# Softmax attentions of a decoder on one core: the order of steps picked by a running estimate of engines, banks and operands

## The reference

```
# layer 0, "mixed": 16 heads of 16; own keys (causal) and the context's keys, both added
y  = softmax(causal(q k^T * scale)) v
y += softmax(qc kc^T * scale) vc            # kc, vc of the 1601 context rows
x  = LN(x + y Wp + bp)
# layer 1: _mha twice, 16 heads of 32, each followed by an MLP
a = softmax(q k^T / sqrt(32));  if causal: a = a * (t > s)   # mask after the softmax
x_out = x + (a v) li1_w + li1_b
```

## Time and profile before

| what | value |
|---|---|
| median of 3 runs | 3924.6 us (3923.4 to 3930.83) |
| the profiled execution | 3913.16 us, its span 3911.8 us |
| linear attention, up to about | 205 us |
| mixed attention | 205 to 1250 us |
| experts and state space | 1250 to 1511 us |
| a1 | 1511 to 2036 us |
| its MLP | 2036 to 2184 us |
| a2 | 2184 to 3203 us |
| its MLP, feed-forward | 3203 to 3912 us |
| PE busy | 3400.6 us, 87% of the span |

### The profile page before, as it was taken

How to read it: one execution, slowest core, us unless ns; L and a number is a source line. 1 busy time by engine, 2 the same in 40 slices (tenths; PEclk the granted TensorE clock), 3 DMA queues, 4 the chain that set the end, 5 groups by cost and what they waited for, 6 DMA issues and landing times. The chain is left out here.

```text
span 3911.8 us, 59055 instructions
## 1 busy us (share of the span) xinstructions
PE 3400.6 (87%) x22156; PEld 2103.2 (54%) x22156; DVE 2247.2 (57%) x4065; ACT 1678.2 (43%) x3067; POOL 983.1 (25%) x1030
## 2 busy tenths in 40 slices
PE   6788989989997974787868599999999987899998
PEld 3443443444433853454547455655556536787787
DVE  6748668676682346555427677676676615433432
ACT  1125646556475321343335055555555544222222
POOL 1100100000101013333334255655555553100000
PEclk9979999999998986898989799999999998999999
DMA  1012211212121313544421443434434402122211
GB/s 70 10 40 50 65 39 47 61 47 70 37 53 56 133 32 60 78 63 64 60 74 41 70 59 57 67 56 64 73 53 61 60 7 88 47 84 70 64 59 55
DMA packets 144628, 229.42 MB, mean 59 GB/s; under 512 B 40917, under 2 KB 90841, under 8 KB 141401
## 3 DMA queue, kind: packets, MB, share of 16 engines
q1 hardware_dynamic: 129048, 216.21, 26.3%
q10 hardware_dynamic: 15296, 9.45, 1.3%
HBM read 99.39 MB, written 8.91 MB: 28 GB/s over the span
## 5 line engine op out<-in xcount | busy, mean ns | idle before, releaser
L958 DVE TENSOR_REDUCE a_mp<-bank 128x1 f32<-128x384 f32 (+2 forms) x1280 | 701.5, 591 | 414.5 <-PE bank L808 401.8
L916 ACT ACTIVATE a_p<-bank 128x512 f32<-128x512 f32 (+1 forms) x1088 | 593.1, 596 | 567.1 <-PE bank L833 460.5
L916 ACT ACTIVATE mx_p<-bank 128x512 f32<-128x512 f32 (+3 forms) x1088 | 548.0, 557 | 403.2 <-PE bank L839 199.4
L958 DVE TENSOR_REDUCE mx_mp<-bank 128x2 f32<-128x768 f32 (+4 forms) x640 | 589.6, 954 | 175.2 <-PE bank L808 99.3
L994 POOL TENSOR_TENSOR a_pair<-a_p 128x512 f32<-128x512 f32 x384 | 491.4, 1309 | 430.8 <-ACT a_p L916 426.8
L808 PE MATMUL bank<-a_ks,a_qs 126*128 126x384 f32 (+2 forms) x1280 | 438.9, 410 | 90.2 <-issue 46.3
L833 PE MATMUL bank<-a_qs,a_ks 128*128 128x512 f32 (+1 forms) x1088 | 392.4, 438 | 25.9 <-DMA a_qs<-a_mt 20.5
L808 PEld LDWEIGHTS bank<-a_ks,a_qs 126*128 126x128 f32 x1280 | 246.2, 197 | 245.9 <-issue 135.4
L222 POOL TENSOR_TENSOR rs<-ve,neghalf 128x4 f32<-128x4 f32 (+2 forms) x80 | 78.1, 976 | 1158.8 <-DVE ve L217 1115.2
L833 PE MATMUL bank<-mx_qs,mx_ks 64*128 64x512 f32 (+3 forms) x1088 | 289.9, 462 | 21.8 <-DMA mx_qs<-mx_mt 16.0
L808 PE MATMUL bank<-mx_ks,mx_qs 62*128 62x384 f32 (+4 forms) x1280 | 275.7, 408 | 13.0 <-DVE mx_mp L958 11.2
(11 more groups left out here) (311 smaller groups left out, 5552.0 us busy)
## 6 DMA issues: line engine op xcount, KB each, us to landing
sf_raw<-in_h_w SPq DMA_DIRECT2D x64, 512.0 KB, 3.6
a_ks<-a_kh SPq DMA_DIRECT2D x96, 192.0 KB, 4.5
ex_w<-in_L_ffn_w SPq DMA_DIRECT2D x16, 1024.0 KB, 5.1
a_qs<-a_qh SPq DMA_DIRECT2D x64, 256.0 KB, 6.1
mx_ks<-mx_kh SPq DMA_DIRECT2D x192, 48.0 KB, 2.1
a_ks<-a_kl SPq DMA_DIRECT2D x48, 192.0 KB, 5.2
mx_qs<-mx_qh SPq DMA_DIRECT2D x128, 64.0 KB, 2.2
mx_rec<-mx_flat SPq DMA_DIRECT2D x128, 64.0 KB, 2.1
```

Source lines behind the costliest of these rows:

```text
L916: act.activation(probs[place % len(probs)][0:kp, q0:T], self.bank(part, n, kb, h)[0:kp, q0:T], ACT.Exp, scale=scale).then_inc(*self.frees( ...
L958: v.tensor_reduce(best[:, tiled * j:tiled * j + tiled, i, ci], bank[:, 0:w] if tiled == 1 else bank[:, :, 0:w], AX.X, ALU.max).then_inc(*s ...
```

## The change

The jobs, the instructions and their numbers are the same (15552 matmuls in both programs); the slots, tiles and banks are the same. What changes is their order in the three attentions, and with it the order on each engine.

- `attention_steps` keeps a `Pace`: for each engine the time at which it comes free, for a bank when it comes back, for each operand when it is ready. PE's time knows the layout it is in: a step in another layout starts `SWITCH` later. Constants stand for matmul columns, drains, transfer issue, bytes and landing.
- At each point it lists the steps that may come next on PE: the next weigh, values, weights, peak, second half of a stack, turn_tops, stack, or work beside. Each has an estimated start plus a handicap from a table of three policies; the least is taken. Values have a smaller handicap while PE is in columns. The peaks' handicap changes between `search` and `early_search` by `left()`, which is rate and lead as before.
- Steps of other engines (split, tops_turned, result, gather, pair and so on) are kept in `later` and yielded when their estimated time has come, no longer after fixed halves. An `until` list holds steps of the work beside back until what they wait for has been yielded.
- In a1 and a2 weigh is one head for each step, no longer two (`parts`).
- A `Pool` gives the bank that comes back first by the estimate, no longer the one that was given back first.
- The list of mixed attention's jobs is written in another way; the jobs come out in the same order (for each batch the four own jobs, then the four cross jobs).

The core of the diff:

```diff
+COLUMN, SWITCH, WAKE, DRAIN, TAIL = 1 / 2.4, 160, 150, 210, 120
+ISSUE, SENT, LANDING = {"sp": 610, "act": 500}, 0.0098, 900
+Policy = namedtuple("Policy", "act_ahead dve_ahead values more_values totals more_totals search early_search turn stack beside aging rate lead")
+MIXED = Policy(700, 1100, 350, 200, -160, 140, -50, 600, 50, 60, 200, 100, 2.6, 4)
+OWN = Policy(700, 1100, 300, 200, -210, 90, 100, 600, -250, 60, 200, 100, 4.2, 2)
+CROSS = Policy(700, 1600, 300, 200, 90, 40, 100, 600, 50, 110, 200, 50, 5.2, 2.5)
...
+class Pace:
+    def __init__(self):
+        self.free, self.mode = defaultdict(float), None
+    def matmul_from(self, mode, ready):
+        start = self.free["pe"] + (SWITCH if mode != self.mode else 0)
+        return max(start, ready + WAKE) if ready > start else start
+    def matmul(self, mode, ns, ready):
+        start = self.matmul_from(mode, ready)
+        self.mode, self.free["pe"] = mode, start + ns
+        return start + ns + DRAIN
+    def run(self, engine, ns, ready):
+        start = max(self.free[engine], ready)
+        self.free[engine] = start + ns
+        return start + ns + TAIL
+    def transfer(self, engine, size, ready):
+        issued = self.run(engine, ISSUE[engine], ready)
+        self.free["queue", engine] = max(self.free["queue", engine], issued) + size * SENT
+        return self.free["queue", engine] + LANDING
...
-    def attention_steps(self, jobs, q_slots, k_slots, tiled, before, during, beside, at_once, after, rate, lead, urgent):
-        blocks = [(n, kb) for n, job in enumerate(jobs) for kb in range(-(-job.nk // P))]
+    def attention_steps(self, jobs, q_slots, k_slots, tiled, before, during, beside, at_once, after, until, load, policy, rooms):
+        side, search, places, raws, recs = rooms
...
+        def weigh_ready(n, kb, part):
+            banks = sorted(bank.back_at for bank in side.idle)[:tiled]
+            return max(ready["tops", n], ready["stack", n, cut_of(n, kb)], *banks)
...
+        def left():
+            at = index[weighs[0][1:3]] + weighs[0][3] / parts if weighs else len(blocks)
+            return min((end + policy.rate * max(0, begins[m] - policy.lead - at) for m, end in enumerate(after_job) if begins[m] > at), default=0)
...
+        def candidates():
+            at = index[weighs[0][1:3]] if weighs else len(blocks)
+            start = lambda mode, when: pace.matmul_from(mode, when)
+            if weighs and weigh_allowed(*weighs[0][1:]):
+                yield start(narrow, max(weigh_ready(*weighs[0][1:]), pace.free["act"] - policy.act_ahead)), 0, weighs
+            if values and values_allowed(*values[0][1:]):
+                yield start("columns", values_ready(*values[0][1:3])), policy.values if pace.mode != "columns" else policy.more_values, values
+            if totals and totals_allowed(*totals[0][1:]):
+                yield start("columns", totals_ready(*totals[0][1:])), policy.totals if pace.mode != "columns" else policy.more_totals, totals
+            if flow and ("split", *flow[0][1:3]) in done and (search is not side or len(side.idle) > 1):
+                n, ci, *_ = flow[0][1:]
+                yield start(narrow, max(ready["stack", n, None], ready["stack", n, ci], search.next().back_at, pace.free["dve"] - policy.dve_ahead)), policy.search if len(flow) > left() else policy.early_search, flow
+            if halves:
+                yield start("full", 0), 10, halves
+            elif turns and not side.held and side.idle:
+                yield start("full", max(ready["tops made", turns[0][1]], ready["tops", turns[0][1] - 1] - 600)), policy.turn, turns
+            if stack_allowed() and side.idle:
+                n, ci = stacks[0]
+                yield start("full", ready["parts", source(n, ci)] - 900 if jobs[n].first else 0), policy.stack, stacks
+            if waiting and side.idle and all(until(step) <= done.union(waiting[0][1]) for step in waiting[0][1]):
+                yield start("full", side.next().back_at), policy.beside - policy.aging * (at - waiting[0][0]), waiting
...
+            elif kind == "split":
+                ci, = at
+                w = T if ci is None else job.cuts[ci][1]
+                low = due
+                if job.first:
+                    low = pace.run("dve", 75 + w / 0.96, due)
+                    self.took[("q", n) if ci is None else ("k", n, ci)][0].back_at = low
+                for _ in range(3 * tiled):
+                    end = pace.transfer("sp", P * HG * w * 4 // (4 * tiled * tiled), low)
+                ready["stack", n, ci] = ready["parts", source(n, ci)] = end
...
+            able = list(candidates())
+            if not able:
+                yield from flush(min(entry[0] for entry in later if may_go(entry)))
+                continue
+            start, _, steps = min(able, key=lambda x: (x[0] + x[1], x[1]))
+            yield from flush(start + 300)
...
-            for part in range(2):
-                yield "weigh", n, kb, part
...
-                heads = (2 * half, 2 * half + 1)
+                heads = range(tiled * part_of, tiled * part_of + tiled)
...
-        jobs = [job(b, kind, h) for b in range(NB) for kind in ("self", "cross") for h in range(NG)]
+        jobs = [job(b, kind, 2 * pair + i) for b in range(NB) for kind in ("self", "cross") for pair in range(NG // 2) for i in range(2)]
...
```

430 lines of the change are left out of this document (287 added, 143 removed).

## The result

| | before | now |
|---|---|---|
| median | 3927.7 us (4 runs, 3923.4 to 3934.8) | 3883.4 us (4 runs, 3877.1 to 3892.4) |
| ratio | | 0.989, 95% interval 0.986 to 0.992 |
| mixed attention | 1070.4 us | 1028.4 us |
| a1 | 530.0 us | 512.5 us |
| a2 | 1044.5 us | 1076.1 us |

The kernel is 44 us faster, not 156. Mixed attention gave half of its 83 us, a1 18 of 80, and a2 lost 32 where 7 were charged. Stages come from the profiled executions, of which before's was 15 us under its median and the changed kernel's, 3892.4 us, 9 us above; so the stages show 21 us of the 44, and the other 23 can't be placed.

A forecast was written before the change was run, and what follows sets the result against it. The prediction took PE's queue as the bound, busy 3400.6 of 3911.8 us. Its terms summed to -156 us, taking 3913.2 to 3757, scaled to 3768 and taken as 3765, with a range of 3670 to 3860.

The forecast's parts named there:

- The keys' waits in a1: In a1, peaks wait for their keys' transfers; more work between split and peak saves 42 of 46.3 us.
- Ends of batches: In mixed attention, the product `Wp,y` waits 31.7 us for POOL; issuing `flat` and `rec` at once saves 18.
- the slower rival: SP's in-order queue blocks splits behind each job's chain in mixed attention and a2: +65 us, 3990; chance 0.06.
- DVE as the bound: In mixed attention DVE becomes the bound, losing half the stage's gain: +40, 3805; case of 3830 to 3890 had 0.12.
- the layout's total in mixed attention: In mixed attention, fewer changes of layout on PE, at 0.10 to 0.20 us per part, save 55 us.
- The turns' term: In a1, turns stand further behind the last peak, saving 10 of 20.8 us of waits.
- The bound that was named: In a1, the keys' three transfers queue behind the queries' three, limiting the saving on peaks' waits to 20 us.
- The clock: Fewer gaps keep PE at the 2.4 GHz level: -12 us in a1, -6 in mixed attention.
- The -15: In a2, one head at a time spreads weigh and peak, sparing 15 us of waits for DVE and ACT.
- The layout's +22: In a2, 68 more changes of layout each way, at 0.33 us for both ways, cost 22 us.
- The warning sign in the prediction: If a2 loses more than 30 us, a layout change in full work costs more than 0.33 us both ways.
- it does not do what it says, around 3880: Estimates drift, vanished waits return elsewhere, only the layout gain of 45 us stays; 3880 fell in a 0.12 case.

The follow-up runs named there:

- half_maxima: queue_bank with mixed attention's maxima taken over only the first half of each score's columns, leaving out half of that search: 3723.3 us.
- queue_bank: The changed kernel with one transfer queue for SP and ACT in the estimate and times for banks of work beside, a2 in its new order: 3758.0 us.
- Late_inverse: The changed kernel with one estimate term moved in a1 alone: a job's inverse counts as possible 5.5 us later than thin's estimated landing: 3837.8 us.
- one_queue: The changed kernel with the estimate letting SP's and ACT's transfers share one queue instead of one each: 3841.2 us.

## Why the prediction was wrong

**The steps that held.** The counts of layout changes and their price: mixed attention's 0.31 for rows to full and back, for which the prediction shows no row, was measured as 0.32, 0.21 out of sums as 0.21, 0.12 into them as 0.09. The keys' waits in a1 (-42): the 46.3 us are gone. Ends of batches (-18): 31.7 to 12.2. Turned maxima in mixed attention (-12): 16.0 to nothing. Two waits went further than forecast: turns in mixed attention, -18 for -4, and turned maxima in a1, -14 for -4. SP's blocking in mixed attention, the slower rival, did not come; no peak there waits for keys. DVE as the bound did not come either (half_maxima).

**What stays open: the layout's total in mixed attention (-55).** PE's busy time there, in which these changes lie, fell by 21 us in the changed kernel and by 35 in queue_bank. Short waits also lie in busy time (27 us of half_maxima's gain did), so no run tells how much of the missing 20 is price and how much is waits.

**The step that failed first: nothing was charged for what the moved chain waits for in a1.** The prediction followed the chain thin, inverse, flat, rec on SP in mixed attention and asked which splits stand behind it. In a1 the same chain is on ACT and DVE, and was not looked at, though the earlier trace rows has 20.8 us of turns behind DVE. The turns' term (-10) turned into +19, and peaks got 17.5 us for ACT. Late_inverse shows the size, 46 us, with one term moved; one_queue gives 57. The bound that was named, that the keys' transfers queue behind the queries', is the very train of six transfers, but its price was looked for at the peaks, and it fell on an 8 KB transfer behind the train.

**The second: no term for banks.** "A Pool gives the bank that comes back first by the estimate" stood in the change, and no step asked whether the estimate knows all banks. It does not, and that costs 43 us in mixed attention, 24 in a1 and 4 in a2. PE's rows in the change can't show it, since they don't say which bank a matmul writes; `account` could, whose first branch returns without a `back_at`.

**The clock (-18)** did not come in a1 (0.89 as before) because the gaps stayed; it did with them gone (0.95). In mixed attention it rose from 0.94 to 0.96.

**a2 (+7) was +32.** The -15 for waits that one head at a time should have spared did not come: DVE's waits before peaks went from 15.9 to 12.7 us, and weigh got some of its own (14.8 us idle, 9.3 before). The layout's +22 stands between 14 (0.20 for both ways) and 22. The warning sign in the prediction, that a loss over 30 us would mean a higher price, is refuted: the price is not higher, and order costs the rest. What of the order was not settled: neither fewer changes nor weigh by pairs wins back more than 6 us.

**The sum.** With both flaws mended and a2 as changed the kernel runs in 3758.0 us; forecast were 3765. By stage it is 983, 435 and 1072 us, where the forecast comes to 987, 450 and 1052. Mending the two flaws gave 125 us. That the mended kernel comes within 7 us of the forecast is partly luck: a1 is 15 us better and a2 20 worse, and in mixed attention waits fell further and busy time less than forecast. The rival "it does not do what it says, around 3880" gave the time and the reason, waits that come back elsewhere, but named no place, and its 3880 fell in a case that had 0.12.

## What to carry to other kernels

When a scheduler's estimate sets the order, read the estimate as part of the change: for each resource ask whether every user of it is entered (here banks of side work were not) and whether what is kept apart in it is apart on the chip (here SP's and ACT's transfers were not). Then look for small in-order steps that wait for a transfer ahead of work that PE wants; 0.25 us of DVE behind 8 KB held up 5 us of PE. And a change that brings under a third of what its own counts say is worth mending before it is judged: two edits of a few lines took it from 1.1% to 4.2%, and a2's old order and another policy to 5.3%.
